# First tiles of 32 rows in four column groups, and weights split only for experts with further tiles

## The reference

```
bids = sigmoid(z @ conf_w.T + conf_b) * wealth     # 8 bids for each token
top two experts; their weights = softmax of their bids
y_e = (silu(z @ gate_e.T) * (z @ up_e.T)) @ down_e.T     # 256 -> 1024 -> 256
x + tanh(g_ffn) * (sum over the two experts of weight * y_e)
```

## Time and profile before

| what | value |
|---|---|
| median of 3 runs | 1134.77 us (1130.64 to 1135.57) |
| span of the profiled execution | 1132.2 us; its own time is one of the three above, which one is not noted |
| PE busy | 1064.4 us, 94% |
| PE weight loads | 889.4 us, 79% |
| DVE, ACT, POOL busy | 650.5, 547.2, 370.9 us |
| DMA | 79.69 MB, 70 GB/s over the span |

### The profile page before, as it was taken

The page is one execution under the profiler, slowest core; times in us unless marked ns, Lnnn a source line. Parts: engine busy times, 40 slices in busy tenths (PEclk is TensorE's granted clock), DMA queues, the critical chain, the costliest instruction groups (busy, mean ns, idle before and its releaser), DMA issues.

```text
span 1132.2 us, 24433 instructions
## 1 busy us (share of the span) xinstructions
PE 1064.4 (94%) x8310; PEld 889.4 (79%) x8310; DVE 650.5 (57%) x1577; ACT 547.2 (48%) x877; POOL 370.9 (33%) x444
## 2 busy tenths in 40 slices
PE   5799999999999978799999999999999999999994
PEld 4566677777777755475999999999679999999993
DVE  3657777877777764357444444444754444454442
ACT  4467777777777744346323333333643332333331
POOL 1223555555545542513212212212322121221221
PEclk8899999999999999999999999999999999999997
DMA  8010111111111173466312112112561121211211
GB/s 243 26 30 21 41 41 52 54 39 39 48 39 39 52 272 147 145 250 204 88 19 38 34 24 38 31 26 38 166 233 25 33 38 19 38 34 24 39 27 23
DMA packets 48698, 79.69 MB, mean 70 GB/s; under 512 B 6416, under 2 KB 42512, under 8 KB 44816
## 3 DMA queue, kind: packets, MB, share of 16 engines
q0 software_dynamic: 18080, 50.93, 16.7%
q1 hardware_dynamic: 30576, 28.23, 8.6%
HBM read 53.69 MB, written 25.18 MB: 70 GB/s over the span
## 4 chain that ended last, share of the span: by engine, by line
PE 82%; ACT 6%; DVE 3%; issue 3%; POOL 3%; DMA 2%; SPq 1%; POOLq 0%; ACTq 0%; DVEq 0%
PE up L1456 16%; PE gate L1456 16%; PE down L1468 10%; PE down L1470 5%; PE pv L583 4%; PE scores L572 4%; PE scores L533 3%; PE misc L479 3%; PE maxps L547 2%; PE gate L1502 2%; PE down L1521 2%; PE up L1502 2%; PE misc L506 2%; PE misc L515 2%; ACT probs L764 2%
## 5 line engine op out<-in xcount | busy, mean ns | idle before, releaser
L1853 POOL DMA_INDIRECT out<-y,token x64 | 101.2, 1581 | 450.3 <-DVE y L1724 351.7
L1617 ACT ACTIVATE silu<-gate 128x512 f32<-128x512 f32 x128 | 76.7, 600 | 277.3 <-PE up L1456 277.3
L1715 DVE TENSOR_TENSOR h<-silu,up 128x512 f32<-128x512 f32 x128 | 88.0, 688 | 179.4 <-ACT silu L1617 179.4
L977 DVE TENSOR_REDUCE max_neg<-maxps 128x4 f32<-128x1024 f32 x128 | 156.5, 1222 | 58.7 <-PE maxps L547 58.7
L1468 PE MATMUL down<-w_split,h_hi 128*128 128x512 f32 x512 | 185.8, 398 | 0.0
L1456 PE MATMUL gate<-x_hi,w_split 128*128 128x256 f32 x1024 | 184.4, 282 | 0.0
L1456 PE MATMUL up<-x_hi,w_split 128*128 128x256 f32 x1024 | 183.7, 281 | 0.0
L764 ACT ACTIVATE probs<-scores 128x1024 f32<-128x1024 f32 x124 | 127.3, 1027 | 78.7 <-PE scores L572 77.7
L1456 PEld LDWEIGHTS gate<-x_hi,w_split 128*128 128x128 f32 x1024 | 148.8, 188 | 3.0
L1456 PEld LDWEIGHTS up<-x_hi,w_split 128*128 128x128 f32 x1024 | 147.9, 188 | 0.0
L1470 PE MATMUL down<-w_split,h_lo 128*128 128x256 f32 x512 | 144.1, 282 | 0.0
(11 more groups left out here) (206 smaller groups left out, 1799.2 us busy)
## 6 DMA issues: line engine op xcount, KB each, us to landing
xg<-dispatched SPq DMA_DIRECT2D x40, 272.0 KB, 2.9
stage<-gate_T POOLq DMA_DIRECT2D x10, 1024.0 KB, 7.7
stage<-up_T POOLq DMA_DIRECT2D x10, 1024.0 KB, 9.8
stage<-down_T POOLq DMA_DIRECT2D x10, 1024.0 KB, 11.8
ctxT<-ctxT SPq DMA_DIRECT2D x17, 256.0 KB, 2.9
x_all<-x SPq DMA_DIRECT2D x16, 256.0 KB, 5.2
out<-x_all SPq DMA_DIRECT2D x16, 256.0 KB, 2.1
out<-y,token POOLq DMA_INDIRECT x70, 3.8
```

What stands on the lines that cost most here:

```text
L977: V.tensor_reduce(to, maxps[:], AX.X, ALU.max, negate=True).then_inc(s["max_taken"], 1)
L1617: nc.scalar.activation(silu[pair % 2][:], gate[pair % 2][:], ACT.Silu).then_inc(s_silu, 1)
L1715: V.tensor_tensor(h[pair % 2][:], silu[pair % 2][:], up[pair % 2][:], ALU.mult).then_inc(s_made, 1)
L1853: pool.indirect_dma_start(out, bass.IndirectOffsetOnAxis(token[:, t:t + 1], axis=0), y[:, t, :], None, compute_op=ALU.add).then_inc(s_adde ...
```

## The change

FIRST becomes 32, so an expert's first tile holds 32 rows and `tiles[e]` is ceil((n - 32)/256). EARLY becomes 4: the first tiles of experts 0 to 3 are in the seam, those of 4 to 7 stand where the experts come up, the next one's gate and up ahead of this one's contraction. Four experts' 32 rows are loaded and turned together (two groups). The 32 rows are the stationary operand of a 128x32 column group; four groups take a quarter of the inner columns each (gate, up) or of the output columns (down). So results lie by quarter on the partitions, and are added to `out` seen as rows of 64 (`first_slot`). The split moves out of `first` into `before_rest`, so only experts with further tiles are split, in pieces that follow the pairs of `gate_up`; expert 2's is in the seam. The next load is issued after the first contraction and the split, three experts ahead. The padding of the first rows becomes four DMAs of 32 rows. `silu` and `h` of the further tiles and the slots lie elsewhere in SBUF; `late` takes the PSUM bank of `flip`.

```diff
-FIRST = P
+FIRST = 32
 REGION = TOKENS + TILE
 STAGES = 3
-EARLY = 2
+EARLY = 4
+RAW = 2
+QUARTERS = P // FIRST
+TAIL = 16
...
+        PIECES = PAIRS + 2
+        ORDER = [*range(RAW, EXPERTS), *range(RAW)]
+        def raw_no(e):
+            return e if e >= RAW else e + EXPERTS
+        def pieces_of(of, piece):
+            if piece < PAIRS:
+                return of[:, 0:2 * third].rearrange("p (k n) -> p k n", n=INNER)[:, :, piece * TILE:(piece + 1) * TILE]
+            start = 2 * third + (piece - PAIRS) * (third // 2)
+            return of[:, start:start + third // 2]
...
+            def load_firsts(group):
+                for i in range(QUARTERS):
+                    at = (group * QUARTERS + i) * REGION
+                    sp.dma_start(first_rows[group][i * FIRST:(i + 1) * FIRST], disp[at:at + FIRST, 0:D]).then_inc(s_first_rows, 16)
+                tails = disp.rearrange("(e g) d -> g e d", g=REGION)[0:FIRST, group * QUARTERS:(group + 1) * QUARTERS, D:D + TAIL]
+                for i in range(QUARTERS):
+                    sp.dma_start(first_tail[i * FIRST:(i + 1) * FIRST, group * QUARTERS:(group + 1) * QUARTERS],
+                                 tails).then_inc(s_first_tails, 16)
+            def first(e, r):
+                if e == RAW + 1:
                     sp.wait_ge(s_padded[1], 16 * (EXPERTS // 2))
...
+            def turn_first_rows(group, bank):
+                pe.wait_ge(s_first_rows, 16 * QUARTERS * (group + 1))
+                for c in range(HC):
+                    last = nc.tensor.transpose(bank[:, c, 0:P], first_rows[group][:, c * P:(c + 1) * P], idn[:])
+                last.then_inc(s_first_turned, 1)
+            def first_gate_up(e):
+                pe.wait_ge(s_first_x, e // QUARTERS + 1)
+                if e < EARLY and e >= 2:
+                    pe.wait_ge(s_fh, e - 1)
+                if e > EARLY:
+                    pe.wait_ge(s_fh, e)
+                slot = slice((e % QUARTERS) * FIRST, (e % QUARTERS + 1) * FIRST)
+                for mat in range(2):
+                    wait_stage(pe, e, mat)
+                    w = weights(stages[e % STAGES], mat)
+                    for c in range(HC):
+                        for i in range(QUARTERS):
+                            last = mm(first_bank(e)[i * FIRST:(i + 1) * FIRST, mat, :], first_x[:, e // QUARTERS, c, slot],
+                                      w[:, c, i * TILE:(i + 1) * TILE], start=c == 0, stop=c == HC - 1)
+                last.then_inc(s_fpair, 1)
+            def first_flip(e):
+                pe.wait_ge(s_fh, e + 1)
+                for a in range(2):
+                    last = nc.tensor.transpose(gate[1][:, 0, a * P:(a + 1) * P], first_h[e % 2][:, a * P:(a + 1) * P], idn[:])
+                last.then_inc(s_fflip, 1)
+            def first_contract(e):
+                pe.wait_ge(s_fhT, e + 1)
+                wait_stage(pe, e, 2)
+                if e > 0:
+                    pe.wait_ge(s_fy, e)
+                w = weights(stages[e % STAGES], 2)
+                cols = D // QUARTERS
+                for k in range(IC):
+                    for i in range(QUARTERS):
+                        last = mm(up[1][i * FIRST:(i + 1) * FIRST, 0, 0:cols], first_hT[:, k % 2, (k // 2) * FIRST:(k // 2 + 1) * FIRST],
+                                  w[:, k, i * cols:(i + 1) * cols], start=k == 0, stop=k == IC - 1)
+                last.then_inc(s_fdown, 1)
...
+            def gate_up(e, pair, r):
+                pe.wait_ge(s_made, r * PAIRS + (pair + 1))
+                pe.wait_ge(s_split[e], pair + 1)
+                if pair == 1:
+                    pe.wait_ge(s_fy, firsts_by(e))
...
+            def first(e):
+                if e == EARLY - 1:
+                    turn_first_rows(1, late)
+                    first_gate_up(EARLY)
+                if e >= EARLY:
+                    first_flip(e)
+                    if e + 1 < EXPERTS:
+                        first_gate_up(e + 1)
+                    first_contract(e)
...
             pe.wait_ge(s["unit_read"], handed["units"])
+            turn_first_rows(0, turned)
             turn_last_normed()
+            last_out()
+            ranks_of_next_to_last()
+            first_gate_up(0)
+            first_gate_up(1)
+            first_flip(0)
             turn_last_x2()
             last_logits()
+            first_contract(0)
+            first_flip(1)
             last_ranks()
+            first_contract(1)
+            first_gate_up(2)
             count_rows()
+            first_flip(2)
+            first_contract(2)
+            first_gate_up(3)
+            first_flip(3)
+            first_contract(3)
+            turn_rows(2)
+            over_tiles_hinted(pe, "pe_count", first, rest)
...
+            def read_first_rows(group, bank):
+                act.wait_ge(s_first_turned, group + 1)
+                nc.scalar.activation(first_x[:, group], bank[:, :, 0:P], ACT.Copy).then_inc(s_first_x, 1)
+            def silu_of_first(e):
+                act.wait_ge(s_fpair, e + 1)
+                nc.scalar.activation(first_silu[e % 2][:], first_bank(e)[:, 0, :], ACT.Silu).then_inc(s_fsilu, 1)
+            def read_first_flip(e):
+                act.wait_ge(s_fflip, e + 1)
+                nc.scalar.activation(first_hT[:].rearrange("p a b -> p (a b)"), gate[1][:, 0, :], ACT.Copy).then_inc(s_fhT, 1)
+            def round_piece(e, piece):
+                n = raw_no(e)
+                for mat in ((0, 1) if piece < PAIRS else (2,)):
+                    wait_stage(act, n, mat)
+                nc.scalar.activation(pieces_of(hi, piece), pieces_of(stages[n % STAGES], piece), ACT.Copy).then_inc(s_hi[e], 1)
...
             def before_rest(e, r):
+                if e != RAW:
+                    for piece in range(PIECES):
+                        if piece == PAIRS:
+                            act.wait_ge(s_y, r * TT + TT)
+                        round_piece(e, piece)
+            def first(e, r):
+                if e == EARLY - 1:
+                    read_first_rows(1, late)
+                    silu_of_first(EARLY)
+                if e >= EARLY:
+                    read_first_flip(e)
+                    if e + 1 < EXPERTS:
+                        silu_of_first(e + 1)
...
+            read_first_rows(0, turned)
             out_of_last()
+            next_to_last_second_weight()
+            silu_of_first(0)
             norm_last()
+            silu_of_first(1)
+            read_first_flip(0)
             read_last_x2()
+            act.wait_ge(s_made, 2)
+            nc.scalar.activation(note[:, 8:9], note[:, 4:5], ACT.Exp)
             last_sigmoid()
+            read_first_flip(1)
             last_second_weight()
+            silu_of_first(2)
+            read_first_flip(2)
+            for piece in range(PIECES):
+                round_piece(RAW, piece)
+            silu_of_first(3)
+            read_first_flip(3)
+            high_of_rows(1)
             over_tiles(act, "act_count", first, rest, before_rest)
...
+            def slots_of_firsts(group):
+                dve.wait_ge(s_first_tails, 16 * QUARTERS * (group + 1))
+                of = slice(group * QUARTERS, (group + 1) * QUARTERS)
+                V.tensor_copy(first_token[:, of], first_tail[:, of, TOKCOL - D].bitcast(i32)).then_inc(s_slots, 1)
+                dve.wait_ge(s_slots, 3 * group + 1)
+                V.scalar_tensor_tensor(first_token[:, of], first_token[:, of], float(QUARTERS),
+                                       quarter[:].to_broadcast([P, QUARTERS]), ALU.mult, ALU.add).then_inc(s_slots, 1)
+                dve.wait_ge(s_slots, 3 * group + 2)
+                V.tensor_copy(first_slot[:, of], first_token[:, of]).then_inc(s_slots, 1)
+            def h_of_first(e):
+                dve.wait_ge(s_fsilu, e + 1)
+                V.tensor_tensor(first_h[e % 2][:], first_silu[e % 2][:], first_bank(e)[:, 1, :], ALU.mult).then_inc(s_fh, 1)
+            def y_of_first(e):
+                dve.wait_ge(s_fdown, e + 1)
+                V.tensor_scalar(first_y[:, e, :], up[1][:, 0, 0:D // QUARTERS], first_tail[:, e, e:e + 1], None,
+                                ALU.mult).then_inc(s_fy, 1)
+            def rest_of_piece(e, piece):
+                dve.wait_ge(s_hi[e], piece + 1)
+                V.tensor_tensor(pieces_of(lo, piece), pieces_of(stages[raw_no(e) % STAGES], piece),
+                                pieces_of(hi, piece).bitcast(fp32), ALU.subtract).then_inc(s_split[e], 1)
...
             def before_rest(e, r):
+                if e != RAW:
+                    for piece in range(PIECES):
+                        rest_of_piece(e, piece)
+            def first(e, r):
+                if e == EARLY - 1:
+                    slots_of_firsts(1)
+                    h_of_first(EARLY)
+                if e >= EARLY:
+                    if e + 1 < EXPERTS:
+                        h_of_first(e + 1)
+                    y_of_first(e)
...
             out_of_last()
```

(55 more changed lines are left out.)

481 lines of the change are left out of this document (120 added, 361 removed).

## The result

The changed kernel took 1107.38 us in the median of 4 runs (1102.83 to 1110.75), the kernel before beside it 1134.9 us; the ratio is 0.975 (0.972 to 0.978). Forecast were 1088, at most 1102. The sign and the kind of the gain were right, its size was not: 27.5 us instead of 47. The profiled execution took 1108.67 us, with a span of 1107.0 us against 1132.2 us before; the sum of the prediction had put that span at 1085.3, so 21.7 us are to be found.

A forecast was written before the change was run, and what follows sets the result against it. TensorE bounds the kernel, so time must come from between its further tiles. Gains of 26.8 (switch to 7), 16.9 (switch to 4) and 5.2 (seam), less 2.0 (low clock), make 46.9 us: 1134.77 to 1088, range 1077 to 1102.

The forecast's parts named there:

- the tile count: Further tiles of experts 2, 4 and 7: 32 in all before and after, 17.42 us each.
- the two switches: Between experts' further tiles: to expert 4 9.2 us, gain 16.9, less 2.0 for low clock; to expert 7 10.5 us, gain 26.8.
- a wait ahead of gate_up(2): At each switch, TensorE waits for the first h, which VectorE makes after five other split pieces: 1.2 us.
- The seam: Behind the attention: weight loads hold the last scatters, row load issued at 480, expert 2's further tile at 487; net gain 5.2.
- The low clock: TensorE idles some 6 us before expert 2's further tile, so the clock falls: 2.0 us charged to that tile.
- Gate and up at 1.1 us: New first tile on TensorE: gate and up are 16 matmuls, priced from the attention's value product at 1.1 us.
- The contraction: New first tile on TensorE: 32 matmuls of 64 columns, bound by weight loads, 1.3 us taken from 1.25 to 2.1.
- The bare split: At each switch the split no longer stands under a first tile, delaying gate_up(0): +1.8 us (expert 7), 1.9 (expert 4).
- A: Seam: weight loads don't hold the scatters, so expert 2's further tile starts near 480.7, 6.3 us sooner; 1082, chance 0.12.
- B: Switch to expert 4: load 5 comes late for gate_up(5), behind adds 0 to 3; priced 8 us, 1096, chance 0.15.
- D: Further tiles: the tile count is not kept, expert 2 gets a second tile, +17.4 us; 1106, chance 0.03.
- C: TensorE's small work is dearer: contractions 3.5 us (+2.2 four times), low clock through both switches some 5 more; 1102, chance 0.14.

The follow-up runs named there:

- no_branch: Changed kernel with TensorE's tests and further-tile loops of experts 0, 1, 3, 5 and 6 left out; 1094.9 us, ratio 0.964.
- no_hint: Changed kernel with all branches kept but without TensorE's branch hints; 1106.6 us, ratio 0.976.
- load5: Changed kernel, loads of experts 4 and 5 behind first and second row copies; one TensorE test jumps to code without tests of 3, 5, 6; 1089.8 us.
- few_first: load5 with the two TensorE versions swapped, so it falls through into the one without tests of experts 3, 5 and 6; 1087.2 us, ratio 0.956.
- between_no_branch: no_branch with the load of expert 4 moved behind GpSimd's first copy of rows; 1090.8 us, ratio 0.960.
- warm: between_no_branch plus 20 unread TensorE matmuls ahead of the turn of expert 2's rows; 1091.4 us, ratio 0.960.
- load5_warm: load5 plus 16 unread matmuls behind expert 3's gate and up and 16 behind its contraction; 1095.3 us, ratio 0.964.
- few_first_warm: few_first plus 16 unread matmuls behind expert 3's gate and up and 10 behind its contraction; 1082.5 us, ratio 0.952.
- double_gate: no_branch with gate and up of expert 6's first tile computed twice; 1100.2 us in one execution.

## Why the prediction was wrong

**What bounds the kernel, the tile count, what the change removes: right.** The gain stands between the tiles, the 32 remain, and with the tests cut the two switches take 9.3 and 11.1 us. The forecast's 9.2 + 2.0 and 10.5 hold 1.2 us each for a wait ahead of gate_up(2), which lies behind these stretches: up to the first gate it was 8.0 + 2.0 and 9.3, so the switches are 0.7 under and 1.8 over it. The mechanism of the column groups was right.

**The step that failed first: TensorE's own program was not in the sum.** The part on the switches adds up matmuls and waits of the engines, and takes it that TensorE goes from one first tile to the next at once. Between them stands the test "has this expert further tiles", with a loop of over 130 matmuls to be jumped over. Before, the hint was given ahead of 12.4 us of matmuls and the jump showed as 0.18 and 0.57 us; a first tile of 3 us doesn't cover it. It cost 3.69 and 4.55 us, and then more, since the clock fell behind the idle: together 4.1 us at the switch to 4 and 9.2 up to the end of the span (each against no_branch), 13.3 of the 21.7. The Trainium skill, page "Runtime: NRT & Kernel Launch", section "Instruction fetch mechanics", has the rule that I passed over: a taken branch whose target lies outside the pages held near the engine makes it wait for a fetch. By it the switches would have been dearer than my sum, and the runs bear that out, with 3.3 to 3.6 us a jump over one loop (no_hint) and 4.9 over the whole nest (load5), and nothing where TensorE falls through (few_first). That the jump is what costs is shown; that it is a fetch stands in the Trainium skill and is not shown.

**The seam: mechanism right, two of its steps wrong.** The loads of experts 3 and 4 hold the last scatters, as forecast. The first wrong step is "The four small firsts (2.7 us each) lie beside it". SyncE's pads were put at 465, from the kernel before, and came at 469.36: 1.7 us of that are an attention that ended later in this execution (its last store at 450.96, before 449.25), the rest a chain of logits, ranks and counts that has grown from 16.3 to 18.4 us between that store and the pads; I had it 1.0 shorter. Up to the last masks it is shorter, by 0.6. But the count stands 5.7 us behind them (467.40) in place of 2.9, since TensorE does the contraction of expert 1 (1.94 us) and gate and up of expert 2 (2.81 us), both partly at the lower clock, ahead of it. The second is what shares the DMAs' time. From the pads to the row load I allowed 15 us and it took 19.5. I priced the two loads alone, 6.3 MB at 425 GB/s, and gave the pads (8 of 272 KB, 2.2 MB) about 1 us; from the first load's issue at 460.45 to 488.2 the DMA view counts 9.3 MB at a mean of 334 GB/s. The second load, forecast for 461.6 and landed by 475, went out at 465.21 and its last third landed at 481. I let SyncE's pads land 1 us behind the scatters, and SyncE waited 4.3 us more for them. From 480 to 488.85 that is 8.9. The low clock was right in kind: 2.0 charged, the tile 19.9 in place of 17.4, so 2.5.

**Gate and up at 1.1 us: a term mis-sized.** The row "x16, 1.07 us" of the earlier trace rows counts instructions, and an fp32 matmul of the program is two of them. The 16 matmuls of a first tile are 32 instructions, at the same price each 1.75 us. On the path that is +0.65 four times, two at each switch, and it was made good elsewhere: the wait of 1.2 us ahead of gate_up(2) came as 0.25 or not at all, and the 2.0 of low clock at the switch to 4 were not lost in no_branch. The contraction took 1.07 to 1.33 us where 1.3 was taken, but by luck: I counted 32 instructions at 0.039 us each, and there are 64 at 0.017. The bare split, +1.8 and +1.9, measured 2.13 to 2.40.

**Rivals.** A did not come true: with both loads in front, pads took 13.7 us, with both behind 4.5. B did not come true in the changed kernel (no wait for stage tiles ahead of gate_up(5)), and did as soon as the seam was shorter. D's 1106 is nearest to the result by luck, since the second tile is not there. C's 1102 is next, but hardly for its reason: its contractions of 3.5 us took 1.07 to 1.33, and its low clock at the switches came behind the jumps. With these gone, TensorE's clock stayed up through both switches (0 us lost there), though they are nothing but small matmuls and short waits; no_branch, columns as above:

```profile
515.29:524.63 9.34, 5.51 (x135) 3.30 (x133) 4.57 (x12) 4.00 (x7) 4.42 (x5) 1.00 0.60 196
...
786.43:797.54 11.11, 8.05 (x264) 5.58 (x263) 4.72 (x11) 4.87 (x9) 3.76 (x3) 0.97 0.33 53
```

It fell right behind the second: expert 7's first gate took 2.70 us (797.54 to 800.24) where the third took 1.43, so 1.3 us in place of the 5 that C had for both. This is no matter of one run: in all eight kernels without these tests (no_branch, between_no_branch, warm, load5, load5_warm, few_first, few_first_warm, double_gate) the clock stands at 0.50 for about 3 or 6 us at the end of the switch to 7 or right behind it, and in four of them (between_no_branch, warm, load5, few_first) for about 3 us at that to 4. Expert 4's 15 tiles take 262.7 to 262.8 us where it falls and 261.8 where it doesn't, so 0.9 us. The Trainium skill's rule on bursts with waits between them (page "TensorE: Matmul & The Clock Gate", section "HAM oscillation") so holds in kind, but the runs put small prices on it: behind the second switch always, behind the first in half of the runs. The page tells it of waits longer than the bursts, which the prediction left out; the waits in no_branch's switches are 0.42 to 2.39 us. Earlier in a switch the clock fell only where a jump or late weights had left TensorE idle for 2.4 to 4.6 us.

**The range** ended at 1102 since every case in it was priced on matmuls, DMAs and clock; a cost of the program's flow was in none.

## What to carry to other kernels

When a piece of work is made much shorter, list what it covered that is no work of any engine: tests, jumps over large bodies and hints, on each engine's own instruction stream; an "issue" idle of near zero before says that it was covered, not that it is free. Put the common case where the program falls through. Price everything that shares the DMA engines with a bulk load, not the bulk alone. And when bulk loads are moved on one queue, follow the small transfers of all queues beside them: a load that no longer holds the scatters may hold the row load, and when that is mended, the next load's own place in the queue decides.
